# Attention and token mixing in one software pipeline: the output projection in quarters, mixing pieces at other places of VectorE's step, POOL's product per score tile

## What is computed

```python
x = x + cross_attention(layernorm(x), ctx)      # 16 heads of 64, softmax over 257 rows, Wo, bo
x = x + mixing(layernorm(x))                    # k, v, r from x and the token before; decayed sums over time
x = x + moe(layernorm(x))                       # 8 experts, argmax routing, 128 -> 512 -> 128
# mixing, per head h of 8 channels, exp_w and exp_u per head:
f_a = exp(k) * v / alpha_next_pow;  f_b = exp(k).sum(-1) / alpha_next_pow
state_a, state_b = alpha_pow * exclusive_cumsum(f_a), alpha_pow * exclusive_cumsum(f_b)
wkv = (state_a + exp_u * exp(k) * v) / max(state_b + exp_u * exp(k).sum(-1), 1e-6)
out = (sigmoid(r) * wkv) @ W_output.T
```

## Time and profile before

| | us |
|---|---|
| median of 3 runs | 1172.28 |
| lowest, highest | 1165.08, 1172.73 |
| the profiled execution | 1169.27 |
| its span, first to last instruction | 1167.5 |

### The profile page before, as it was taken

One profiled execution on the slowest core, in us unless ns is written; L12 is line 12 of the kernel. 1 busy time (PEld: TensorE's weight loads), 2 busy tenths in 40 slices (PEclk: granted clock), 3 DMA queues, 4 the chain that ended last, 5 costly groups with the idle time before them and its releaser, 6 DMA issues.

```text
span 1167.5 us, 31247 instructions
## 1 busy us (share of the span) xinstructions
PE 935.8 (80%) x9098; PEld 772.6 (66%) x9099; DVE 832.9 (71%) x2229; ACT 731.2 (63%) x2072; POOL 687.1 (59%) x1194
## 2 busy tenths in 40 slices
PE   4799888888988898989797989888897628228885
PEld 3688777776767676767676777677676517226664
DVE  5677687888787868787878877888877655415553
ACT  2587777676767676767676767667676412226664
POOL 3275667666666666666666666666666430645454
PEclk9899999999999999999999999999999955659897
DMA  6000000000000000000000000000000090111110
GB/s 178 1 17 28 15 16 15 15 15 14 14 14 17 24 14 14 14 14 14 14 14 14 14 14 14 14 14 14 14 15 2 25 231 1 45 49 46 43 43 17
DMA packets 46499, 32.27 MB, mean 28 GB/s; under 512 B 6518, under 2 KB 44065, under 8 KB 46448
## 3 DMA queue, kind: packets, MB, share of 16 engines
q1 hardware_dynamic: 44144, 27.38, 9.2%
q0 software_dynamic: 2304, 4.25, 1.1%
HBM read 24.62 MB, written 7.52 MB: 28 GB/s over the span
## 4 chain that ended last, share of the span: by engine, by line
PE 33%; POOL 25%; issue 20%; ACT 9%; DVE 8%; POOLq 1%; DMA 1%; ACTq 1%; SPq 1%; DVEq 0%
POOL Pn L750 11%; PE bank L411 7%; PE bank L388 4%; PE bank L425 4%; PE bank L1269 3%; POOL chi L732 3%; ACT Pe L555 2%; PE bank L432 2%; PE bank L1284 2%; POOL sorted_rows L1073 2%; ACT Th L547 2%; POOL e12p L757 1%; DVE nmax L633 1%; PE bank L917 1%; PE bank L400 1%
## 5 line engine op out<-in xcount | busy, mean ns | idle before, releaser
L750 POOL TENSOR_TENSOR Pn<-Pe,rsum 128x1028 f32<-128x1028 f32 x128 | 246.5, 1926 | 258.5 <-DVE rsum L643 220.3
L555 ACT ACTIVATE Pe<-bank,nmax 128x257 f32<-128x257 f32 x512 | 240.0, 475 | 88.8 <-DVE nmax L633 88.4
L388 PE MATMUL bank<-cT,qh 96*128 96x257 f16 x1024 | 187.2, 277 | 95.3 <-ACT Pe L555 92.4
L633 DVE TENSOR_REDUCE nmax<-bank 128x1 f32<-128x257 f32 x512 | 203.3, 412 | 42.5 <-PE bank L388 41.1
L629 DVE TENSOR_TENSOR Tl<-bank,Th 128x512 f16<-128x512 f32 x256 | 173.7, 679 | 0.4 <-ACT Th L547 0.4
L547 ACT ACTIVATE Th<-bank 128x512 f16<-128x512 f32 x256 | 141.2, 593 | 49.8 <-PE bank L432 48.4
L388 PEld LDWEIGHTS bank<-cT,qh 96*128 96x128 f16 x1024 | 84.7, 98 | 119.7 <-ACT Pe L555 90.4
L432 PE MATMUL bank<-identf,Pn 128*128 128x128 f32 x1024 | 147.8, 273 | 0.0
L388 PE MATMUL bank<-cT,ql 96*128 96x257 f16 x512 | 140.5, 274 | 0.0
L432 PEld LDWEIGHTS bank<-identf,Pn 128*128 128x128 f32 x1024 | 115.0, 142 | 5.9
L616 DVE TENSOR_TENSOR ql<-bank,qh 96x512 f16<-96x512 f32 x128 | 87.8, 686 | 31.7 <-ACT qh L611 31.7
(11 more groups left out here) (238 smaller groups left out, 2601.0 us busy)
## 6 DMA issues: line engine op xcount, KB each, us to landing
raw<-in_ctx_dram SPq DMA_DIRECT2D x32, 384.0 KB, 3.2
sorted_rows<-fill SPq DMA_DIRECT2D x1, 2620.0 KB, 18.2
xs<-sorted_rows SPq DMA_DIRECT2D x40, 65.5 KB, 1.8
R<-in_x_dram SPq DMA_DIRECT2D x4, 512.0 KB, 5.7
Z<-last_rows SPq DMA_DIRECT2D x128, 2.2 KB
w1r<-in_L_ffn_W_dram SPq DMA_DIRECT2D x8, 256.0 KB, 6.1
w2fr<-in_L_ffn_W_dram SPq DMA_DIRECT2D x8, 256.0 KB, 6.4
out_dram<-yout,idx POOLq DMA_INDIRECT x40, 2.3
```

The costliest lines, as they stand in the source:

```text
L388: last = nc.tensor.matmul(bank[SB[t]][:, 0:M], w[:, par, b, t * P:(t + 1) * P], cT[:, s4, c, 0:M], start=(k == 0), stop=(k == 2))
L555: nc.scalar.activation(Pe[:, n_par(j + 1), t, :], bank[SB[t]][:, 0:M], ACT.Exp, bias=nmax[:, n_par(j + 1), t:t + 1], accum_out=sums[:, n_p ...
L633: nc.vector.tensor_reduce(nmax[:, n_par(j + 1), t:t + 1], bank[SB[t]][:, 0:M], AX.X, ALU.max, negate=True).then_inc(s_nmax, 1)
L750: nc.gpsimd.tensor_tensor(Pn[:, par, :, :], Pe[:, par, :, :], rsum[:, par, :].unsqueeze(2).broadcast_to([P, QT, M]), ALU.mult)\
```

## The change

Three parts, and what they bring with them:

1. pe_y does a quarter of a group's projection (4 heads, 12 matmuls) in every step, behind q and ahead of the fourth score tile. Each quarter is its own accumulation, and VectorE adds each to R. TensorE waits for that addition at the head of the next step, ahead of the context transposes.
2. On VectorE mixing pieces stand at three places of the step: ahead of the last maximum (dve_mix_a, and the moments), between ql and rsum (dve_mix_b), and at the end (dve_mix_end). Scans are done four at a time, clamp and mask for one of the two states a step, the state of the sums first, and num apart from den.
3. POOL's product is four instructions of one score tile each; waits on s_pn count four per sequence.

The pieces of the other engines move to fitting steps, so a chunk's transposes come at j = -1 of the next iteration instead of j = 4, and everything behind them later. The pipeline has three more steps behind the last sequence, and drain_mix begins three steps later.

```diff
-        def pe_y(g, gp):
-            wait(nc.tensor, s_Ol, GB * (g + 1))
-            for h in range(H):
+        def pe_y(n, part, par):
+            wait(nc.tensor, s_res, n - 5)
+            for h in range(part * QT, part * QT + QT):
...
@@ pe_step
-            if jj == 2 and exists(g - 1, G):
-                wait(nc.tensor, s_res, g)
             if exists(n + 2):
+                if exists(n - 6):
+                    wait(nc.tensor, s_res, n - 5)
                 pe_ctxT(n + 2, (j + 2) % NC8, (j + 2) % 4)
...
+            if exists(n - 5):
+                if exists(n + 2):
+                    wait(nc.tensor, s_cT, n + 3)
+                else:
+                    wait(nc.tensor, s_L12, min(n, B))
+                if jj == 1:
+                    wait(nc.tensor, s_Ol, GB * g)
+                pe_y(n, (jj + 3) % GB, gp if jj == 0 else 1 - gp)
             if exists(n + 1):
                 pe_scores(n + 1, ((j + 1) // GB) % NP2, (j + 1) % GB, (j + 1) % 4, (3,))
...
-            if jj == 1 and exists(g - 1, G):
-                pe_y(g - 1, 1 - gp)
...
-                wait(nc.tensor, s_pn, n + 1)
+                wait(nc.tensor, s_pn, QT * (n + 1))
@@ dve_step, inside the loop over maxima and Tl
+                if t == 3:
...
+                    dve_stat(it, j, g, jj, gp)
+                    dve_mix_a(it, j)
...
             if exists(n + 5):
                 dve_q(n + 5, (gp + 1 + (jj + 1) // GB) % NP2, (j + 1) % GB)
+            if jj == 1 and exists(g - 2, G):
+                nc.vector.bn_aggr(mv[:, gp, :], stats2[:, gp, :]).then_inc(s_m["mv"], 1)
+            dve_mix_b(it, j)
...
+            if exists(n - 5):
+                wait(nc.vector, s_y, n - 4)
+                tile = X[:, bass.ds(g - (2 if jj == 0 else 1), 1), :].rearrange("p o c -> p (o c)")
                 nc.vector.tensor_tensor(tile, tile, bank[7][:, 512 - C:512], ALU.add).then_inc(s_res, 1)
...
-            dve_mix(it, j)
+            dve_mix_end(it, j)
@@ new functions of VectorE, by their steps
+        def dve_mix_a(it, j):
+            if j in (3, 4) and chunk(it, 2) is not None:
+                dve_scans(it - 2, j - 3, 0)
+            if j in (5, 6) and chunk(it, 2) is not None:
+                dve_state(it - 2, j - 5)
+        def dve_mix_b(it, j):
+            if j in (3, 4) and chunk(it, 2) is not None:
+                dve_scans(it - 2, j - 3, 1)
+            if j == 5 and chunk(it, 2) is not None:
...
+            if j == 6 and chunk(it, 2) is not None:
...
+            if j == -1 and chunk(it, 3) is not None:
...
+        def dve_mix_end(it, j):
...
@@ pool_step
-                nc.gpsimd.tensor_tensor(Pn[:, par, :, :], Pe[:, par, :, :],
-                                        rsum[:, par, :].unsqueeze(2).broadcast_to([P, QT, M]), ALU.mult)\
-                    .then_inc(s_pn, 1)
+                for t in range(QT):
+                    nc.gpsimd.tensor_tensor(Pn[:, par, t, :], Pe[:, par, t, :],
+                                            rsum[:, par, t:t + 1].broadcast_to([P, M]), ALU.mult).then_inc(s_pn, 1)
```

More of the change, by code:

```diff
@@ L499, in pe_mix @@
         def pe_mix(it, j, n):
-            if j == 4 and chunk(it, 1) is not None:
-                c = it - 1
+            if j == -1 and chunk(it, 2) is not None:
+                c = it - 2
                 pe_mix_bank(it, j, n)
@@ L513, in pe_mix @@
                     .then_inc(s_m["k"], 1)
-            if j == 6 and chunk(it, 1) is not None:
-                c = it - 1
+            if j == 4 and chunk(it, 3) is not None:
+                c = it - 3
+                pe_mix_bank(it, j, n)
+                wait(nc.tensor, s_m["o"], c + 1)
+                for t in range(MG):
+                    last = nc.tensor.matmul(bank[3][:, t * P:(t + 1) * P], oT[:, t * P:(t + 1) * P],
+                                            w2T[:, 3, :], start=True, stop=True)
+                last.then_inc(s_m["y"], 1)
+            if j == 1 and chunk(it, 2) is not None:
+                c = it - 2
                 pe_mix_bank(it, j, n)
@@ L528, in pe_mix @@
                 nc.tensor.matmul(bank[3][:, 0:MT], w2T[:, 2, :], xm[:, 1, :], start=True, stop=True).then_inc(s_m["r"], 1)
[L529 to L536, removed]
         def n_par(j):
@@ L669, in dve_mix, with dve_scans @@
                                        X[:, bass.ds(MG * c + t, 1), :].rearrange("p o c -> p (o c)")).then_inc(s_m["stat3"], 1)
-            if j == -1 and chunk(it, 2) is not None:
+        def dve_scans(c, k, half):
+            wait(nc.vector, s_m["st"], 2 * c - 1 + k)
+            wait(nc.vector, s_m["fab"], 2 * c + 1 + k)
+            for b in range(half * MS // 2, (half + 1) * MS // 2):
+                last = nc.vector.tensor_tensor_scan(cs[:, 1 - k, b, 1:N + 1], onesn[:, :],
+                                                    fab[:, 1 - k, b * N:(b + 1) * N], 0.0, ALU.mult, ALU.add)
+            last.then_inc(s_m["cs"], 1)
@@ L671, in dve_mix @@
+        def dve_mix_end(it, j):
+            if j == 4 and chunk(it, 3) is not None:
+                c = it - 3
+                wait(nc.vector, s_m["y"], c + 1)
+                xc = X[:, bass.ds(MG * c, MG), :]
+                nc.vector.tensor_tensor(xc, xc, bank[3][:, 0:MT].rearrange("p (t c) -> p t c", t=MG), ALU.add)\
+                    .then_inc(s_m["res"], 1)
+            if j == 2 and chunk(it, 2) is not None:
                 c = it - 2
@@ L685, in dve_mix @@
[L685 to L697, removed]
-                wait(nc.vector, s_m["num"], c)
-                for k in range(2):
-                    wait(nc.vector, s_m["scl"], 2 * c + k + 1)
-                    nc.vector.scalar_tensor_tensor(sst[:, k, :], sraw[:, k, :], FMAX, scl[:, k, :],
-                                                   ALU.is_le, ALU.mult).then_inc(s_m["sst"], 1)
@@ L718, in dve_mix @@
-            if j == 5 and chunk(it, 2) is not None:
-                c = it - 2
-                wait(nc.vector, s_m["o"], c)
-                wait(nc.vector, s_m["dm"], c + 1)
-                nc.vector.reciprocal(rec[:, :], denm[:, :]).then_inc(s_m["rec"], 1)
         def dve_cT(n, s4):
```

199 lines of the change are left out of this document (104 added, 95 removed).

## The result

The changed kernel takes 1102.26 us (median of 4 runs, 1100.14 to 1103.77) against 1170.67; the ratio is 0.942, 95% interval 0.938 to 0.946. The profiled execution took 1102.80, 66.5 us less than the one of before, where 74 were forecast; its span, first to last instruction, is 1100.1.

The account below looks back on a forecast made before the run. No engine is full; TensorE and VectorE have long steps in turn with little buffering. Thirteen iterations 5.2 us shorter (67) plus 7 make 74 off 1169.3, so 1095 us (chance 0.62), range 1065 to 1140.

Parts of the forecast that it names:

- Two kinds of long steps that hold each other up: Attention iteration: TensorE's projection (2.68 us) and VectorE's mixing lengthen different steps, each engine waiting for the other; 55.36 us.
- An iteration of 50.2 us: Eight attention steps, each at the longer of TensorE and VectorE, plus allowances: 50.2 us, 5.2 less than before.
- 1.8 us of allowances: Added to the iteration's step sum of 48.4 us: 0.8 us of remaining coupling and 1 us for new blocks.
- no step above 7 us: Sign that the forecast is right: in iterations of 49 to 51.5 us, no step exceeds 7 us.
- 67 and 7 us of gain: Pipeline: thirteen iterations gain 5.2 us each, 67; the two where mixing sets in gain 7 together; the first gains 0.
- The quarter costs 0.67 us and stands in a hole: TensorE ahead of the fourth score tile: 12 matmuls take 0.67 us, free where VectorE's long steps leave a 0.82 us hole.
- VectorE's base and pieces, 43.2 us: VectorE's busy time per iteration: 45.00 less 3.5 of lengthening plus 1.7 of added residuals, 43.2 us; base 4.17 a step.
- POOL's product: +0.55 us a step, "cost nothing": Four product tiles on POOL add 0.55 us a step, at no cost within TensorE's 3.1 us slack.
- Rival (a), the residual's wait: VectorE gates every step, pieces delaying TensorE's next head; some 3 us idle, 53.4 us an iteration, 1140; chance 0.17.
- the sign of (a): TensorE idle ahead of the context transposes until a residual addition; about 3 us an iteration.
- Rival (c), the port: VectorE's pieces and POOL's product tiles block each other by the shared port: 60.6 us an iteration, 1237; chance 0.04.
- The end, 0 between -3 and +5: Dependent mixing behind the last product, 41 us before: change taken as 0, between -3 and +5 us.

Follow-up runs that it names:

- experiment 7: Changed kernel with one product instruction, whole projection and VectorE's mixing pieces at the step's end, its plan of steps kept: 1175.66 us, ratio 1.0075 to the kernel before.
- experiment 4: Changed kernel with the projection quarter moved behind the product with V, ahead of the transpose of e12p: 1106.53 us, ratio 0.950 to the kernel before.
- experiment 1: Changed kernel with POOL's product back in one instruction instead of four: 1081.47 us, ratio 0.926 to the kernel before.
- experiment 9: Changed kernel with POOL's product in two instructions of two score tiles each: 1087.48 us, ratio 0.930 to the kernel before.
- experiment 10: One-product version of the changed kernel with dve_mix_b moved from ahead of the reciprocal of the sums to behind the residual addition: 1128.14 us, ratio 0.967.
- experiment 12: One-product version of the changed kernel, residual addition right behind ql and TensorE waiting for it ahead of the transpose of e12p: 1106.23 us, ratio 0.949.
- experiment 11: Changed kernel, product in four tiles, with dve_mix_b moved from ahead of the reciprocal of the sums to behind the residual addition: 1110.01 us, ratio 0.950.
- experiment 3: Changed kernel with the whole projection of 48 matmuls back in a group's second step, one residual addition per group: 1119.58 us, ratio 0.959.

## Why the prediction was right

The forecast was 1095 in a range of 1065 to 1140; 1102 was measured. Part of that closeness is luck: two errors went against each other. The split, priced at nothing, cost 21 us, and without it the kernel takes 1081, 14 us under the forecast. Point by point:

- **Two kinds of long steps that hold each other up.** Right: shown by experiment 7 and the table. Undoing projection and places together with one product brings back 94 us and nearly all of TensorE's wait for Pe (89.1 of 92.4 us).
- **An iteration of 50.2 us.** 50.6 measured. By the forecast of steps, which without its 1.8 us of allowances is 48.4: 6.9 against 7.2 (j = 5), 5.5 against 5.8 (6), 6.2 against 6.9 (-1); j = 0 and 1 together 12.15 against 11.9; 5.85 against 5.7 (2), but 5.9 against 6.8 (3) and 5.9 against 6.4 (4). The two steps with scans are the worst misses, and the sign "no step above 7 us" failed narrowly, with 7.2 and 7.1. Half-clock stretches added 1.1 to 1.6 us to each of four iterations, which the sum had left out.
- **67 and 7 us of gain.** The pipeline got 71 us shorter in these two executions: 61 in the thirteen later iterations (the last of them has seven steps), 8.4 in the two in which mixing sets in, 1.8 in the first, which was put at 0. The setup took 2.7 back and the end 0.8.
- **The quarter costs 0.67 us and stands in a hole.** The 0.67 is right (620.08 to 620.75 in the timeline). The hole is worth little: experiment 4 gives 4 to 8 us for it.
- **VectorE's base and pieces, 43.2 us.** Right for one product (43.34); 44.47 with four tiles. The 1 us kept for new blocks was the right size on VectorE (1.1), and its cause is the split.
- **POOL's product: +0.55 us a step, "cost nothing".** This is the step that failed. The size was 0.43 us (2.33 against 1.90), and TensorE's slack for the product did hold: it waited 0.8 us in all for e12p. POOL's heaviest step, put at 6.1 us, took 6.7 (product to product, 642.96 to 649.65, without a gap). But what follows the product on POOL moved too, fab and sraw onto VectorE's scans and masks, and xn at the end of the iteration by as much. I looked only for who waits for the product, not for who shares a port with what is queued behind it. It cost 21 us of total time: 0.8 us of each iteration, some 10 us, by the path just named (experiments 1 and 9); the rest isn't taken apart.
- **Rival (a), the residual's wait.** 28.9 us in 27 waits, 2.2 us an iteration or 0.28 a step, inside the price of 0 to 0.4; mostly one wait of 1.5 to 1.7 us at the step with den and denm. So the sign of (a) was seen, with 2.2 of its 3 us, but not its time: the kernel of experiment 1 waits the same 28.9 us and takes 1081. Experiments 10 and 12 show that the obvious ways out of it cost more.
- **Rival (c), the port.** The mechanism is real, the size small: 16 us of VectorE's time in all.
- **The end, 0 between -3 and +5.** +0.9 measured.
- **Slips in the sums.** 43.4 + 2.9 is 46.3, not 46.2, and 3 us on top of 50.2 make rival (a) 53.2, not 53.4. Neither changes the forecast or the range.

The Trainium skill (SBUF — State Buffer, "SBUF: two separate sides") describes a lock: of a GpSimd instruction and a VectorE instruction of certain kinds, the one that starts first holds the port pair for its whole length, and the other waits. The traces agree, with den's 2.01 us beside a product of 1.90 in experiment 10, and experiment 11 shows its other face: shorter holds shorten the longest block but meet more instructions.

## What to carry to other kernels

Where two engines have their long steps in turn with little buffering, spread the work of both. The gains don't add: with one product the places alone gave 75 us, the quarters alone 46, both 94; and the second remedy for the same loss, here the split, gave little or harmed. Before an instruction is split to shorten the time for which it blocks another engine, check whether the blocked pieces still stand beside it: on this kernel the split was worth 14 us with the pieces beside the product and minus 21 once they had moved. Of a step that gets longer, look at everything queued behind it, and at who shares a port with that. The version to keep is that of experiment 1, 1081 us, which beats both kernels.

## What the runs showed of the hardware that was not expected

Short instructions suffer from short holds: with dve_mix_b beside four tiles a scan of 32 elements averaged 406 ns, beside one long product 376, with both groups away from the product 223 to 233. And the moment at which setup's matmuls go from 0.31 to 0.22 us moved between 38 and 49 us over executions of kernels whose setup is the same, and in two of them (experiments 3 and 9) it did not come before 64 us. In the twelve whose setup matmuls began at 36 to 37 us, the reciprocal ahead of the first product stood between 56.7 and 63.2 us, which alone shifts a time by up to 6.5 us, more than a small edit does. Last, TensorE's granted clock fell to 0.50 for 3.4 us behind waits of 1.66 to 2.01 us in the changed kernel (four of its thirteen such waits), and not once in the pipeline of experiment 1, where all but one of the waits at that place are 1.2 to 1.25. The kernel before has three such stretches without that wait, so it isn't the only cause, and that it is one is not shown by a run.
